# Full attention: SyncE issues the transfers of the maxima's rows, and the maxima are turned three steps before a group's end

## The chip, the cores and the metric

The program runs on one core of a Trainium2 chip. The metric is the device time of one launch, in microseconds (us). Engines: PE is TensorE (PEld its weight loads), DVE is VectorE, ACT is ScalarE, POOL is GpSimd, SP is SyncE, which in this kernel only issues transfers.

## What is computed

Four layers on 4 sequences of 1024 tokens with 128 channels: full attention, an expert feed-forward layer, causal full attention, and a stack of windowed attention and feed-forward layers. The change is inside the two full attentions (the second is causal), which have 16 heads of 8 channels:

```python
scores = jnp.einsum('bhtd,bhsd->bhts', q, k) * scale
attn = jax.nn.softmax(scores.astype(jnp.float32), axis=-1).astype(q.dtype)   # first one
y = jnp.einsum('bhts,bhsd->bhtd', attn, v)
...
scores = jnp.where(causal, scores, -jnp.inf)                                 # second one
attn = jax.nn.softmax(scores / jnp.sqrt(jnp.float32(hd)), axis=-1)
ctx = jnp.einsum('bhqk,bhkd->bhqd', attn, v)
```

## The kernel before

`attention` is called twice, with tags `a1` (not causal) and `a2` (causal). It works on 16 groups (`GROUPS`), each of 4 heads (`GH`) of one sequence. A softmax needs each query's largest score before the exponentials. So every group is gone through twice.

The first pass finds the maxima. For each chunk of 128 queries by up to 512 keys PE multiplies (L456, tile `a_pr`, three PSUM banks used in turn) and DVE takes the largest value per query (L371, into `a_mpart`). There are 64 chunks per group in `a1`, all 512 keys wide, and 48 in `a2`, 128 to 512 wide. Then `finish_maxima` (L376) merges them into the column tile `a_mcol`, PE turns that into rows (`turn_maxima`, L466), and DVE splits the rows into three bf16 parts (L380 to L386, tile `a_mrow`, semaphore `m_split`). Three transfers put them into three spare rows of the group's query tile `a_QS` (`rows_of`, L591, semaphore `m_stored`). With the matching rows of -1 in `a_KS` the second product gives scores minus their maximum.

The second pass makes the output in steps. In `a1` there are 16 steps per group (NS), one for each half of the queries (512) and each block of 128 keys. In `a2` there are 12 steps, with 512, 384, 256 and 128 queries in steps 0 to 3, 512 in steps 4 to 8, and 384, 256 and 128 in steps 9 to 11. A step has scores for two pairs of heads (PE, L474, tile `a_ps`), two exponentials (ACT, L612, tile `a_probs`), and the weighting by the values (PE, L492, tile `a_po`). PE computes the scores of step s+1 inside step s.

The two passes are interleaved by hand: while group g's steps run, the chunks of the group that comes next are spread over them. `turn_steps` gives the order in which steps get chunks: before, the last two steps of the group before (NS-2 and NS-1), then steps 0 to NS-3. The last of that order gets none. After it the maxima are turned. In `a1` the shares are 4 or 5 chunks a step and step 13 has none. In `a2` step 9 has none. Each engine runs its queue in order:

- ACT calls `rows_of` ahead of the exponentials of step NS-2. It waits there for `m_split` and issues the three transfers.
- PE waits for `m_stored` at the start of step NS-1, whose first work is the scores of the next group's step 0.
- SP loads a group's operands (L324 to L326) into one of three buffers once all scores of the group that held the buffer are computed.
- PE's chunk k+3 waits until DVE has read chunk k, for there are three banks. The turned maxima and the turned outputs take a place in the same round of banks.

Of the kernel before, what the change touches and what calls it, by code (L numbers as in the profile page):

```python
# [18 lines left out]
P = 128  # L19
# [221 lines left out]
def attention(nc, A, tag, vals, attn, q_parts, k_parts, ident, causal):  # L241

    PAIRED, BUFS = 2, 3
    with ExitStack() as ctx:
# [32 lines left out]

        turn_steps = [NS - 2, NS - 1, *range(NS - 2)]
        room = [CH - steps[s][2] for s in turn_steps[:NS - 1]]
# [9 lines left out]
        for s in turn_steps:  # L289
            ring += [("chunk", k) for k in share[s]]  # L290
            if s == 1:
                ring.append(("out", 0))
            if s == ends[0] + 1:
                ring.append(("out", 1))
            if s == NS - 3:
                ring.append(("rows", 0))
# [18 lines left out]
        with nc.Block() as block:  # L315
            @block.sync
            def _(sp):
                sp.dma_start(cmask[:, :, :], A["c_causal"]).then_inc(consts, 16)
                sp.wait_ge(zeroed, 4 + FIRST)
                qg = q_parts.rearrange("(g h d) j t -> g (d j) h t", h=GH, d=HD)  # L320
                kg = k_parts.rearrange("(g h d) j t -> g (d j) h t", h=GH, d=HD)

                def load(g, b):
                    sp.dma_start(QS[0:KROWS, b, :, :], qg[g, :, :, :]).then_inc(operands[b], 16)  # L324
                    sp.dma_start(KS[0:KROWS, b, :, :], kg[g, :, :, :]).then_inc(operands[b], 16)
                    sp.dma_start(QS[KROWS:KROWS + 3, b, :, :], norows[:, :, :]).then_inc(operands[b], 16)  # L326

                for g in range(BUFS):
                    load(g, g)
                for g in range(BUFS, GROUPS + 1):  # L330
                    sp.wait_ge(scores, 2 * NS * (g - BUFS + 1) + FIRST)
                    load(g % GROUPS, g % BUFS)

            @block.gpsimd
# [21 lines left out]
            def _(dve):  # L356
# [49 lines left out]
                def step(s, g, v):  # L406
                    if s == 2:
                        normalise(g * 2 - 1, 1, place((g + (GROUPS - 1)) % GROUPS))
                    if s == ends[0] + 2:
                        normalise(g * 2, 0, place(g))  # L410
                    for k in share[s]:
                        half_max(k, v + 1)
                    if s == NS - 3:
                        finish_maxima(v + 1)
# [3 lines left out]
                finish_maxima(0)  # L418
                for s in (NS - 2, NS - 1):
                    for k in share[s]:  # L420
                        half_max(k, 1)
                for s in range(NS - 2):
                    step(s, 0, 0)
                with dve.Fori(0, (GROUPS - 1) // BUFS) as i:
                    for b in range(BUFS):
                        v = i * BUFS + (b + 1)
                        for s in turn_steps:
                            step(s, v - 1 if s >= NS - 2 else v, v)
                normalise(GROUPS * 2 - 1, 1, place(GROUPS - 1))

            @block.tensor
            def _(pe):
# [74 lines left out]
                def step(s, g, b, v, vb, loads):  # L507
                    hq, kt, c0 = steps[s]
                    todo = list(share[s])
                    pe.wait_ge(exped, g * (2 * NS) + (2 * s + 1) + FIRST)  # L510
                    if s == NS - 2:
                        pe.wait_ge(operands[vb], loads * 48)
# [23 lines left out]
                    if s == ends[0] + 1:  # L536
                        turn_out(g * 2, 1, g)
                    if s == NS - 3:
                        turn_maxima(v + 1)
# [8 lines left out]
                pe.wait_ge(operands[1], 48)  # L548
                for s in (NS - 2, NS - 1):
                    for k in share[s]:  # L550
# [3 lines left out]
                for pair in range(PAIRED):  # L554
                    score(0, 0, 0, pair)
                for s in range(NS - 2):
                    step(s, 0, 0, 0, 1, 1)
                with nc.Fori(0, (GROUPS - 1) // BUFS, engines=bass.OrderedEngineSet([pe.engine]),
                             hint_back_edge=True) as i:
                    for b in range(BUFS):  # L560
                        v = i * BUFS + (b + 1)
                        for s in turn_steps:
                            if s >= NS - 2:
                                step(s, v - 1, b, v, (b + 2) % BUFS, i + (1 + (b + 2) // BUFS))
                            else:
                                step(s, v, (b + 1) % BUFS, v, (b + 2) % BUFS, None)
                for s in (NS - 2, NS - 1):
                    kt = steps[s][1]
# [16 lines left out]
            def _(act):  # L585
                def rows_of(par, g):

                    act.wait_ge(m_split, g + 1 + FIRST)
                    for j in range(3):
                        r = KROWS + j  # L590
                        act.dma_start(QS[r:r + 1, par, :, :].rearrange("p h t -> p (h t)")  # L591
                                      .rearrange("p (r c) -> p r c", c=P),
                                      mrow[:, j, :]).then_inc(m_stored, 16)

                def keep_out(u, before):
# [4 lines left out]
                def step(s, g, b):  # L600
                    hq, kt, c0 = steps[s]
                    if s == NS - 2:
                        rows_of((b + 1) % BUFS, g + 1)
                    for pair in range(PAIRED):
# [11 lines left out]
                act.wait_ge(ones_set, 1 + FIRST)  # L616
                rows_of(0, 0)
                for s in range(NS):
# [5 lines left out]
                keep_out(GROUPS * 2 - 1, GROUPS * NS)  # L624
                act.wait_ge(m_stored, (GROUPS + 1) * 48)

# [1424 lines left out]
```

## Time and profile before

| | us |
|---|---|
| Time, median of 3 runs (6683.9 to 6689.47) | 6685.75 |
| The profiled execution's own time | 6694.51 |
| Its span | 6692.6 |
| PE busy in it | 5291.4 (79%) |
| DVE busy | 4489.2 (67%) |
| ACT busy | 3324.6 (50%) |
| Mean granted clock of PE | 0.881 |

The profile is of one execution. Times in it count from the start of its span. The first attention's groups run from about 174 to 1104 us, the second's from about 1402 to 2112 us. A timeline row gives start, length, engine, line, operation, the tile written and the tiles read, and how many are merged in the row. In brackets is how long the engine sat idle before the first of them, and what ended that. "issue" says that the profile shows nothing waited for, which also holds where an engine's queue was at a wait or at issuing a transfer that the row doesn't name. ACTq and SPq are transfers issued by ACT and SP. PEclk is the share of full clock that PE was granted (1.00 is 2.4 GHz, 0.50 is 1.2 GHz).

### The profile page before, as it was taken

Reading aid. Unit: us, or ns where it says so; the run is one execution under the profiler, and the core shown is the slowest. Engines: PE = TensorE matmul, PEld = TensorE weight load, DVE = VectorE, ACT = ScalarE, POOL = GpSimd, SP = SyncE. Lnnn points to the kernel's source line nnn. Section 1 sums busy time; section 2 is a strip of 40 time slices with the busy share of each in tenths; the row PEclk is TensorE's granted clock in tenths of the full one; section 3 lists DMA queues with packets and bytes.
Section 4 is the critical chain, followed back from the end, with each engine's and each line's share of the span. In section 5 each row is a group of like instructions: output and inputs, shape, how many; then the busy total and the mean of one; then the engine's idle time right before and its main releaser. Section 6 shows DMA issues by size and latency. Waiting matters only on the chain. (4 is left out here: it accounts for less than half of the span.)

```text
span 6692.6 us, 227324 instructions
## 1 busy us (share of the span) xinstructions
PE 5291.4 (79%) x94976; PEld 3161.9 (47%) x95234; DVE 4489.2 (67%) x9665; ACT 3324.6 (50%) x6837; POOL 2664.5 (40%) x2369
## 2 busy tenths in 40 slices
PE   5888888667776688888888888887888888888876
PEld 1222222223332455555555565565565565565553
DVE  5777775665665567666667666666666666766764
ACT  1555555324443355555555555555555555555543
POOL 0000000000000556655655655655655655655652
PEclk9999998879998788888888888888888888888886
DMA  3000000211011000010001100110001000110000
GB/s 105 11 15 15 15 15 29 77 27 21 17 21 45 20 25 20 24 41 20 24 25 29 31 25 20 31 35 20 24 25 34 25 25 21 32 32 22 21 26 20
DMA packets 88389, 185.96 MB, mean 28 GB/s; under 512 B 18294, under 2 KB 44854, under 8 KB 87606
## 3 DMA queue, kind: packets, MB, share of 16 engines
q1 hardware_dynamic: 83324, 182.95, 10.4%
q8 instruction: 95, 1.56, 0.1%
q10 hardware_dynamic: 4896, 0.84, 0.1%
q14 instruction: 74, 0.61, 0.0%
HBM read 54.14 MB, written 27.26 MB: 12 GB/s over the span
## 5 line engine op out<-in xcount | busy, mean ns | idle before, releaser
L371 DVE TENSOR_REDUCE a_mpart<-a_pr 128x1 f32<-128x512 f32 (+2 forms) x1904 | 1104.8, 628 | 481.6 <-PE a_pr L456 274.2
L612 ACT ACTIVATE a_probs<-a_ps 128x1024 f32<-128x1024 f32 (+3 forms) x896 | 802.1, 932 | 909.2 <-PE a_ps L474 439.8
L1502 ACT ACTIVATE w_probs<-w_pa,w_nm,w_rqs 128x64 f32<-128x64 f32 x3072 | 968.3, 414 | 125.8 <-DVE w_nm L1650 125.8
L1495 ACT ACTIVATE w_sq<-w_pr 128x512 f32<-128x512 f32 x768 | 466.0, 607 | 901.4 <-DVE w_sinb L1638 901.4
L474 PE MATMUL a_ps<-a_QS,a_KS 128*128 128x512 bf16 (+3 forms) x1719 | 501.0, 374 | 276.6 <-ACT a_probs L612 151.9
L1424 PE MATMUL w_pr<-w_xc,w_w 128*128 128x256 f32 (+1 forms) x1152 | 459.5, 580 | 295.9 <-issue 295.9
L456 PE MATMUL a_pr<-a_KS,a_QS 128*128 128x512 bf16 (+3 forms) x1815 | 609.3, 381 | 91.8 <-DMA a_QS<-a_norows 78.2
L1238 POOL TENSOR_TENSOR w_probs<-w_probs,w_rden 128x512 f32<-128x512 f32 x384 | 393.2, 1045 | 541.1 <-DVE w_rden L1660 541.1
L1212 POOL TENSOR_TENSOR w_sinb<-w_sinb,w_tabk 128x512 f32<-128x512 f32 x384 | 488.2, 1271 | 283.9 <-DVE w_sinb L1638 283.9
L338 POOL COPY a_V<-a_vals 128x288 f32 (+1 forms) x32 | 14.3, 455 | 1436.9 <-PE a_po L492 1436.8
L1638 DVE STREAM_SHUFFLE w_sinb<-w_pr 128x512 f32<-128x512 f32 x768 | 562.4, 732 | 0.0
L1384 PE MATMUL w_pa<-w_probsT,w_V 32*64 32x32 f32 x24576 | 502.9, 228 | 16.4 <-issue 16.4
L1547 ACT COPY w_oT<-w_pa 128x512 f32<-128x512 f32 x384 | 197.1, 600 | 634.3 <-PE w_pa L1384 634.3
L1384 PE MATMUL w_pa<-w_probsT,w_Vp 32*64 32x32 f32 x24576 | 501.3, 228 | 11.7 <-issue 11.7
L1424 PEld LDWEIGHTS w_pr<-w_xc,w_w 128*128 128x128 f32 (+1 forms) x1152 | 311.5, 279 | 418.0 <-issue 374.1
L1384 PEld LDWEIGHTS w_pa<-w_probsT,w_Vp 32*64 32x64 f32 x24576 | 486.5, 132 | 33.5 <-issue 33.5
L1220 POOL TENSOR_TENSOR w_ksum<-w_cosb,w_sinb 128x512 f32<-128x512 f32 x384 | 487.7, 1270 | 36.4
L1220 POOL TENSOR_TENSOR w_qT<-w_cosb,w_sinb 128x512 f32<-128x512 f32 x384 | 487.1, 1269 | 36.4
L1212 POOL TENSOR_TENSOR w_sinb<-w_sinb,w_tabq 128x512 f32<-128x512 f32 x384 | 487.0, 1268 | 9.0 <-DVE w_sinb L1638 9.0
L1384 PEld LDWEIGHTS w_pa<-w_probsT,w_V 32*64 32x64 f32 x24576 | 467.2, 132 | 17.6 <-issue 17.6
L492 PE MATMUL a_po<-a_probs,a_V 128*32 128x512 f32 (+3 forms) x3584 | 456.3, 580 | 3.1 <-issue 0.2
L456 PEld LDWEIGHTS a_pr<-a_KS,a_QS 128*128 128x128 bf16 x1904 | 186.0, 102 | 566.2 <-DVE a_mpart L371 357.0
(225 smaller groups left out, 9928.1 us busy)
## 6 DMA issues: line engine op xcount, KB each, us to landing
w_Vp<-w_V SPq DMA_DIRECT2D x192, 384.0 KB, 3.7
w_Vp<-w_V SPq DMA_DIRECT2D x192, 128.0 KB, 3.4
a_QS<-q_parts SPq DMA_DIRECT2D x34, 384.0 KB
a_KS<-k_parts SPq DMA_DIRECT2D x34, 384.0 KB
q_parts<-a1p_part SPq DMA_DIRECT2D x48, 128.0 KB, 1.8
k_parts<-a1p_part SPq DMA_DIRECT2D x48, 128.0 KB, 1.8
q_parts<-a2p_part SPq DMA_DIRECT2D x48, 128.0 KB, 1.8
k_parts<-a2p_part SPq DMA_DIRECT2D x48, 128.0 KB, 1.8
```

Of the source, the lines that this page charges most:

```text
L371: nc.vector.reduce_max(mpart[:, h, qt, kc:kc + 1], p_r[:, at["chunk", k] % 3, 0:width], AX_X).then_inc(max_read, 1)
L456: mm = nc.tensor.matmul(p_r[:, bank, 0:width], QS[:, b, h, qt * P:(qt + 1) * P], KS[:, b, h, kc * CH:kc * CH + width], start=True, stop=True)
L474: mm = nc.tensor.matmul(p_s[:, pair, e, c0:CH], KS[:, b, h, kt * P:(kt + 1) * P], QS[:, b, h, q0:(hq + 1) * CH], start=True, stop=True)
L492: mm = nc.tensor.matmul(p_o[32 * h:32 * h + 32, c0:CH], V[b][:, kt, h, :], probs[:, s % 2, h, c0:CH], start=kt == 0, stop=s in ends, skip_ ...
L612: nc.scalar.activation(probs[:, s % 2, 2 * pair:2 * pair + 2, c0:CH], p_s[:, pair, :, c0:CH], ACT.Exp, scale=SM_SCALE).then_inc(exped, 1)
L1212: nc.gpsimd.tensor_tensor(sinb[:, u % 4, :, :], sinb[:, u % 4, :, :], tab[:, 1:2, :].broadcast_to([P, 2, PAIR]), ALU.mult).then_inc(S[f"si ...
L1220: nc.gpsimd.tensor_tensor((ksum if u < 4 else qT)[:, b:b + 2, :], cosb[:, u % 4, :, :], sinb[:, u % 4, :, :], ALU.add).then_inc(S[f"add{u} ...
L1384: mm = nc.tensor.matmul(o_of(w)[64 * e:64 * e + 64, b, t, :], (V if blk else Vp)[r, t, f:f + DH], probsT[r, 2 * e + gl, t, c, blk, :], sta ...
L1424: mm = nc.tensor.matmul(F_BANK[bank][0:hi - lo, at, :], w1[:, off + lo:off + hi], xc[:, :], start=True, stop=True)
L1495: nc.scalar.square(sq[:, u, :, :], UNIT_BANK[u][:, :, :]).then_inc(S[f"sq{u}"], 1)
L1502: op = nc.scalar.activation(probs[:, g, t, c, :], s_of(g)[:, t, c, :], ACT.Exp, bias=nm[:, g, t, c:c + 1], scale=scale_of(g)[:, t, c:c + 1])
L1638: nc.vector.stream_shuffle(sinb[:, u % 4, :, :].rearrange("p a f -> p (a f)"), UNIT_BANK[u][:, :, :].rearrange("p a f -> p (a f)"), SWAP). ...
```

## The change

`rows_of` moves from ACT's program to SP's. There it stands ahead of the wait for the scores and the load that follow it. A constant LAG = 3 takes the place of the fixed 2: the turn steps are now the last three of the group before and steps 0 to NS-4, so that the step without chunks, and the turn behind it, come one step earlier (step 12 in `a1`, step 8 in `a2`). The wait for a group's operands moves with them to step NS-3; the wait for `m_stored` stays at step NS-1. The final wait for all rows' transfers moves from ACT to SP.

```diff
-    PAIRED, BUFS = 2, 3
+    PAIRED, BUFS, LAG = 2, 3, 3
...
-        turn_steps = [NS - 2, NS - 1, *range(NS - 2)]
+        turn_steps = [*range(NS - LAG, NS), *range(NS - LAG)]
...
-            if s == NS - 3:
+            if s == NS - LAG - 1:
                 ring.append(("rows", 0))
...
+                def rows_of(g):
+                    sp.wait_ge(m_split, g + 1 + FIRST)
+                    for j in range(3):
+                        r = KROWS + j
+                        sp.dma_start(QS[r:r + 1, g % BUFS, :, :].rearrange("p h t -> p (h t)")
+                                      .rearrange("p (r c) -> p r c", c=P),
+                                      mrow[:, j, :]).then_inc(m_stored, 16)
+
                 for g in range(BUFS):
                     load(g, g)
+                rows_of(0)
                 for g in range(BUFS, GROUPS + 1):
+                    rows_of(g - 2)
                     sp.wait_ge(scores, 2 * NS * (g - BUFS + 1) + FIRST)
                     load(g % GROUPS, g % BUFS)
+                rows_of(GROUPS - 1)
+                rows_of(GROUPS)
+                sp.wait_ge(m_stored, (GROUPS + 1) * 48)
...
-                    if s == NS - 3:
+                    if s == NS - LAG - 1:
                         finish_maxima(v + 1)
...
-                    if s == NS - 2:
+                    if s == NS - LAG:
                         pe.wait_ge(operands[vb], loads * 48)
...
-                    if s == NS - 3:
+                    if s == NS - LAG - 1:
                         turn_maxima(v + 1)
...
-                def rows_of(par, g):
-
-                    act.wait_ge(m_split, g + 1 + FIRST)
-                    for j in range(3):
-                        r = KROWS + j
-                        act.dma_start(QS[r:r + 1, par, :, :].rearrange("p h t -> p (h t)")
-                                      .rearrange("p (r c) -> p r c", c=P),
-                                      mrow[:, j, :]).then_inc(m_stored, 16)
...
-                    if s == NS - 2:
-                        rows_of((b + 1) % BUFS, g + 1)
...
-                rows_of(0, 0)
...
-                act.wait_ge(m_stored, (GROUPS + 1) * 48)
```

ACT's queue in `a1`, from its start through the first group. Before (a_osum is the copy of a half's output, a_probs the exponentials):

```order
L591 DMA a_QS<-a_mrow 1x32x128 x3
L612 ACTIVATE a_probs<-a_ps 128x1024
L598 COPY a_osum<-a_po 128x512
L612 ACTIVATE a_probs<-a_ps 128x1024 x16
L598 COPY a_osum<-a_po 128x512
L612 ACTIVATE a_probs<-a_ps 128x1024 x11
L591 DMA a_QS<-a_mrow 1x32x128 x3
L612 ACTIVATE a_probs<-a_ps 128x1024 x4
```

And now:

```order
L614 ACTIVATE a_probs<-a_ps 128x1024
L602 COPY a_osum<-a_po 128x512
L614 ACTIVATE a_probs<-a_ps 128x1024 x16
L602 COPY a_osum<-a_po 128x512
L614 ACTIVATE a_probs<-a_ps 128x1024 x15
```

The transfers that stood ahead of the last two steps' four exponentials are gone, with the wait in front of them.

SP's queue in `a1` after the first three loads, now (before, the loads alone stood there):

```order
L332 DMA a_QS<-a_mrow 1x32x128 x6
L324 DMA a_QS<-q_parts 48x4x1024
L325 DMA a_KS<-k_parts 48x4x1024
L326 DMA a_QS<-a_norows 3x4096
L332 DMA a_QS<-a_mrow 1x32x128 x3
L324 DMA a_QS<-q_parts 48x4x1024
L325 DMA a_KS<-k_parts 48x4x1024
L326 DMA a_QS<-a_norows 3x4096
```

One set of three rows' transfers now stands ahead of each load.

DVE's queue in `a1` from the end of the first group's maxima to the turn of the second's. Before (L371 are the chunks' reductions, L376 to L386 the turn):

```order
L371 TENSOR_REDUCE a_mpart<-a_pr 128x1 x17
L392 RECIPROCAL a_rsum<-a_pr 128x16
L397 TENSOR_TENSOR a_attn<-a_pr,a_rsum 128x4x32
L371 TENSOR_REDUCE a_mpart<-a_pr 128x1 x30
L392 RECIPROCAL a_rsum<-a_pr 128x16
L397 TENSOR_TENSOR a_attn<-a_pr,a_rsum 128x4x32
L371 TENSOR_REDUCE a_mpart<-a_pr 128x1 x17
L376 TENSOR_REDUCE a_mcol<-a_mpart 128x32
L380 CAST a_mrow<-a_pr 32x128
```

And now:

```order
L384 TENSOR_REDUCE a_mpart<-a_pr 128x1 x21
L405 RECIPROCAL a_rsum<-a_pr 128x16
L410 TENSOR_TENSOR a_attn<-a_pr,a_rsum 128x4x32
L384 TENSOR_REDUCE a_mpart<-a_pr 128x1 x30
L405 RECIPROCAL a_rsum<-a_pr 128x16
L410 TENSOR_TENSOR a_attn<-a_pr,a_rsum 128x4x32
L384 TENSOR_REDUCE a_mpart<-a_pr 128x1 x13
L389 TENSOR_REDUCE a_mcol<-a_mpart 128x32
L393 CAST a_mrow<-a_pr 32x128
```

There are 64 reductions either way. Four of them moved from behind the second output to ahead of the first, so the turn comes a step sooner.

## Rows read from the trace of the kernel before

**Rows 1.** Waits of ACT, first attention: engine, line, what it waited for, us, times, longest.

```profile
ACT a_probs L612 <- issue: 90.1, 16, 5.6
```

**Rows 2.** Waits of ACT, second attention.

```profile
ACT a_probs L612 <- issue: 95.7, 16, 6.3
```

**Rows 3.** Timeline of ACT, rows' transfers: groups 0 and 15 of a1, 0 and 9 of a2.

```profile
222.51 1.82 ACTq L591 DMA_DIRECT2D a_QS<-a_mrow  x3
...
1093.83 1.79 ACTq L591 DMA_DIRECT2D a_QS<-a_mrow  x3
...
1437.31 1.81 ACTq L591 DMA_DIRECT2D a_QS<-a_mrow  x3
...
1836.88 1.79 ACTq L591 DMA_DIRECT2D a_QS<-a_mrow  x3
```

**Rows 4.** Timeline of DVE at the end of a group of a1.

```profile
564.52 1.29 DVE L371 TENSOR_REDUCE a_mpart<-a_pr 128x1 f32<-128x512 f32 x2 [0.39 <-PE a_pr L456]
...
568.31 0.69 DVE L371 TENSOR_REDUCE a_mpart<-a_pr 128x1 f32<-128x512 f32 x1 [0.29 <-PE a_pr L456]
...
571.26 0.28 DVE L386 TENSOR_TENSOR a_mrow<-a_mrest,a_mrow 32x128 bf16<-32x128 f32 x1
576.41 1.29 DVE L371 TENSOR_REDUCE a_mpart<-a_pr 128x1 f32<-128x512 f32 x2 [4.87 <-PE a_pr L456]
578.12 0.69 DVE L371 TENSOR_REDUCE a_mpart<-a_pr 128x1 f32<-128x512 f32 x1 [0.42 <-PE a_pr L456]
580.01 2.54 DVE L371 TENSOR_REDUCE a_mpart<-a_pr 128x1 f32<-128x512 f32 x4 [1.21 <-PE a_pr L456]
```

**Rows 5.** Timeline of ACT, PE and SP in the same stretch.

```profile
568.11 1.03 PE L474 MATMUL a_ps<-a_QS,a_KS 128*128 128x512 bf16 x4
...
570.06 0.29 PE L466 MATMUL a_pr<-ident,a_mcol 128*32 128x128 f32 x1
...
573.55 1.94 ACT L612 ACTIVATE a_probs<-a_ps 128x1024 f32<-128x1024 f32 x2 [5.63 <-issue]
...
574.92 1.03 PE L474 MATMUL a_ps<-a_QS,a_KS 128*128 128x512 bf16 x2 [4.57 <-ACT a_probs L612]
...
577.68 0.31 SPq L324 DMA_DIRECT2D a_QS<-q_parts  x1
```

**Rows 6.** Windows: us, each engine's busy time, PEclk, DMA share, GB/s; first one group.

```profile
515.63:573.55 57.92, 50.02 (x260) 14.15 (x265) 42.91 (x73) 32.37 (x34) 0.45 (x1) 0.94 0.09 15
574.90:577.00 2.10, 2.08 (x5) 0.73 (x6) 0.59 (x1) 1.53 (x2) 0.00 (x0) 0.50 0.02 4
579.70:582.00 2.30, 2.30 (x16) 0.66 (x14) 1.99 (x4) 1.02 (x1) 0.00 (x0) 1.00 1.09 175
585.00:590.00 5.00, 5.00 (x31) 1.47 (x29) 4.31 (x8) 3.21 (x4) 0.00 (x0) 1.00 0.00 0
```

**Rows 7.** The rows' transfers, by their tile: us from issue to landing.

```profile
DMA to landing us min/median/max: 1.8/1.9/3.2
```

**Rows 8.** Timeline of ACT, end of a1: its last group's last steps.

```profile
1095.82 1.94 ACT L612 ACTIVATE a_probs<-a_ps 128x1024 f32<-128x1024 f32 x2 [5.62 <-issue]
1098.96 1.94 ACT L612 ACTIVATE a_probs<-a_ps 128x1024 f32<-128x1024 f32 x2 [1.21 <-PE a_ps L474]
```

**Rows 9.** Timeline of DVE and ACT at the end of a group of a2.

```profile
1659.08 0.28 DVE L386 TENSOR_TENSOR a_mrow<-a_mrest,a_mrow 32x128 bf16<-32x128 f32 x1
1663.05 0.51 DVE L371 TENSOR_REDUCE a_mpart<-a_pr 128x1 f32<-128x128 f32 x2 [3.69 <-PE a_pr L459]
...
1667.42 1.02 ACT L612 ACTIVATE a_probs<-a_ps 128x1024 f32<-128x1024 f32 x1 [3.34 <-PE a_ps L478]
1669.77 1.02 DVE L371 TENSOR_REDUCE a_mpart<-a_pr 128x1 f32<-128x384 f32 x2 [1.36 <-PE a_pr L459]
...
1694.99 1.94 ACT L612 ACTIVATE a_probs<-a_ps 128x1024 f32<-128x1024 f32 x2 [1.83 <-PE a_ps L478]
1698.00 1.69 ACT L612 ACTIVATE a_probs<-a_ps 128x768 f32<-128x768 f32 x2 [1.07 <-PE a_ps L478]
```

More of the change, by code:

```diff
@@ L418, in _ @@
                 finish_maxima(0)
-                for s in (NS - 2, NS - 1):
+                for s in range(NS - LAG, NS):
                     for k in share[s]:
                         half_max(k, 1)
-                for s in range(NS - 2):
+                for s in range(NS - LAG):
                     step(s, 0, 0)
@@ L427, in _ @@
                         for s in turn_steps:
-                            step(s, v - 1 if s >= NS - 2 else v, v)
+                            step(s, v - 1 if s >= NS - LAG else v, v)
                 normalise(GROUPS * 2 - 1, 1, place(GROUPS - 1))
@@ L548, in _ @@
                 pe.wait_ge(operands[1], 48)
-                for s in (NS - 2, NS - 1):
+                for s in range(NS - LAG, NS):
                     for k in share[s]:
@@ L555, in _ @@
                     score(0, 0, 0, pair)
-                for s in range(NS - 2):
+                for s in range(NS - LAG):
                     step(s, 0, 0, 0, 1, 1)
@@ L562, in _ @@
                         for s in turn_steps:
-                            if s >= NS - 2:
+                            if s >= NS - LAG:
                                 step(s, v - 1, b, v, (b + 2) % BUFS, i + (1 + (b + 2) // BUFS))
@@ L566, in _ @@
                                 step(s, v, (b + 1) % BUFS, v, (b + 2) % BUFS, None)
-                for s in (NS - 2, NS - 1):
+                for s in range(NS - LAG, NS):
                     kt = steps[s][1]
```

## The prediction

> **What bounds the kernel now.** Only the two full attentions change, so I read them alone. First the waits of ACT: in the first attention its exponentials stood idle 16 times, 90.1 us in all, on "issue" [rows 1]; in the second 16 times, 95.7 us [rows 2]. Sixteen is the number of groups, and 90.1 / 16 = 5.63 us is what one timeline row shows directly ahead of the exponentials of step 14, from 567.92 to 573.55 [rows 5]. That is a wait of ACT's queue for the split maxima, 3.6 us up to 571.54, followed by 1.79 us of issuing three transfers [rows 3, 4]. Next the distance from one group's transfers to the next: (1093.83 - 222.51) / 15 = 58.09 us in a1 and (1836.88 - 1437.31) / 9 = 44.40 us in a2 [rows 3].
>
> Is ACT's stall on the path? ACT is busy only 32.37 us of a group of 57.92, DVE 42.91, PE 50.02 [rows 6]. Away from the boundary DVE's reductions run with gaps of 0.29 to 0.39 us only, and PE is busy all the time [rows 4, 6], so DVE and PE pace the steps together. At the boundary both stop. DVE ends its last chunk at 568.31 + 0.69 = 569.00 and the split at 571.26 + 0.28 = 571.54, and has its next chunk at 576.41, after 4.87 us of nothing [rows 4]. PE stands 4.57 us until ACT's first exponential, which could have started soon after the scores of 568.11 but starts at 573.55 [rows 5]. So the stall is on everyone's path. It also leaves PE at half clock (0.50, 1.2 GHz), where it had 1.00 again from 579.70 on [rows 6]; in that stretch DVE waits another 0.42 and 1.21 us [rows 4].
>
> **The change, part by part.** I call S the moment at which the maxima are split.
>
> *ACT's wait and issues go.* In a1 the exponentials of the step behind the turn follow their scores, PE goes straight on, and the chunks of that step are in their banks while DVE still splits. From 569.00 to the reduction at 580.01 DVE is idle or in the turn for 7.41 + 0.42 + 1.21 = 9.04 us [rows 4]. The turn itself, 2.54 us (569.00 to 571.54), stays, and so does one ordinary gap of 0.39 us. 9.04 - 2.54 - 0.39 = 6.1 us per group. What is late next is again the reductions, at their ordinary pace. Bounds: 4.6 us if only PE's idle time goes and the clock gives nothing back, 6.6 us if the gaps near the turn close too. I take 6.1, the sum of rows, for it leaves each ordinary gap in.
>
> *The turn one step earlier.* It removes no instruction. It gives the transfers two steps with chunks of cover before PE wants them at step NS-1. Three issues take 1.79 us on ACT [rows 3]; I take the same on SP, since its loads' issue rows are of this kind, and landing takes 1.9 us (1.8 to 3.2) [rows 7]: they are in place at S + 3.7, at worst S + 5.0. In a1 a step of four chunks takes 2.53 + 0.39 = 2.9 us and one of five 3.9; PE enters the first when the turn's product is out (570.35 [rows 5]), 1.2 us before S, so it asks at -1.2 + 2.9 + 3.9 = S + 5.6. It does not wait. In front of the transfers SP has only the load of the group before, issued some 50 us earlier and finished within a few us (DMA share 1.09 at 579.7 to 582, 0.00 from 585 on) [rows 6]. Behind them on SP stands the next load, which had to wait for the last scores anyway; it is needed a whole group later.
>
> *a2, where the last steps are narrow.* Before, from S (1659.36) to the first exponential of step 0 (1667.42) it takes 8.06 us, in which steps 10 and 11 have 8 chunks, with DVE idle 3.69 us at once, and 1.36 us once more ahead of step 0's first chunk [rows 9]. After, steps 9, 10 and 11 come behind the turn with 12 chunks: four of 128, four of 256 and four of 384 keys, at 0.26, 0.38 and 0.51 us [rows 9], 4.6 us of reductions. With some 1.4 us of gaps they end at S + 6.0, and the first exponential of step 0 is at about S + 5.7: 2.4 us gained. The rest of the group took 44.40 - 8.06 = 36.3 us. It has one step less now (1698.00 - 1694.99 = 3.0 us [rows 9]) and 0.5 us less of half clock, but one more chunk to reduce (up to 0.9 us), and a widest step without chunks (step 8 in place of 9), whose wider products and weighting delay the turn by 0.4 us. So 2.4 + 3.0 + 0.5 - 0.9 - 0.4 = 4.6, or 5.5 if the chunk fits into gaps; I take 5.0 us per group. Bounds: 3.7 (the 3.69 us gap alone) and 6.5. PE asks for the rows at S + 5.0 here: covered by 1.3 us at the median landing, not at all at the longest.
>
> *The ends.* The last group has no next one's chunks in its last steps. Its stall goes too (5.62 us idle, of which at least 0.9 is the ordinary wait for scores, so 4.7), and about 1 us of slow clock, but one more step runs bare: 1098.96 - 1095.82 = 3.1 us [rows 8]. That is a gain of 2.6 us. At the start four more chunks are reduced before the first step, and one step less runs in the first group, which cancels. The same for a2. SP's final wait for the transfers is over long before the last output.
>
> *Sum.* a1: 15 x 6.1 + 2.6 = 94. a2: 15 x 5.0 + 2.6 = 78. Together 172 us: 6694.5 - 172 = 6522.5 for a profiled execution. That one ran 8.8 us above the median of the runs shown (6685.75), so I forecast 6514 us. The bounds taken together are 15 x (4.6 + 3.7) + 5 = 130 and 15 x (6.6 + 6.5) + 6 = 203: 6556 and 6483.
>
> **Rivals.**
>
> *The wait for the landed rows takes over.* PE asks at S + 5.6 and S + 5.0. If SP needs longer per issue or rows land later than ACT's did, say at S + 7 in both, PE waits 1.4 and 2.0 us, 32 times: 54 us lost, 6568. For it: the longest landing of 3.2 us [rows 7] would use up a2's cover. Against: the median is 1.9, and the load's data moves later.
>
> *Only the issue time is saved.* If the split and the landing stay ahead of the same work, because they bound the group's end all along, just ACT's 1.79 us of issuing goes, 32 times: 57 us, 6629. Against it: PE waits for ACT's exponential, not for a transfer [rows 5], and the turn is moved too. The Trainium skill's page "DMA: Bandwidth & Descriptors", section "Issuing engines are not separate DMA queues", says that the issuing engine only matters for the sequencer's time to initiate a transfer, which is usually small beside the transfer. By that rule this rival would be the forecast; the trace agrees that the transfer itself gets no faster, but shows a wait of 3.6 us in front of the issues that leaves the exponentials' queue with them.
>
> *The gain is larger.* PE and DVE are both near their pace; if the warm clock also closes gaps later in the group, 7.2 us a group are possible: 30 x 7.2 = 216, 6470. For it: half clock reaches into the next group's first steps [rows 6, 9]. Against: from 579.70 on the clock is 1.00.
>
> *Slower: the rows land with the load.* Rows and operands now share SP's queue. SP issues the load once the last scores are done, some 3.5 us behind S by my estimate (it was 577.68 - 574.92 = 2.8 us into the step behind the stall [rows 5]), and its data keeps the DMA engines busy for about 5 us [rows 6]. If rows were only reported landed when that load is through, at about S + 10.5, PE would wait 4.9 us in a1 and 5.5 in a2, at half clock again behind it (1.6 us), and one wait would be traded for another: 6.5 and 7.1 lost against 6.1 and 5.0 gained, 15 x 2.5 = 37 us slower, 6723. It decides from a landing of about S + 9.3 on. Against: the three transfers of 8 KB are issued ahead of the load and take 1.9 us. The Trainium skill's same page, section "Queues, rings and completion order", says that on each DMA engine descriptors are consumed in ring order. By that the rows go first and this rival falls; no row here has both on one queue.
>
> **How the numbers follow.** Forecast 66%, late landing 14%, issue time only 5%, larger gain 12%, slower 3%. The likeliest gives 6514. The range is 6478 to 6562: the bounds of the sum (6483, 6556), widened a little towards the larger gain and the milder part of the late landing. About 0.2% (13 us) can be told from no change. No case lies within it but a mix near the slower one: faster 96%, same 1%, slower 3%.
>
> **What would show it.** Right: ACT has no idle on issue near a group's end; DVE starts the next chunk within 0.2 us of S; PE's clock stays at 1.00 through a group of a1; the distance between groups' transfers is 52.0 us in a1 and 39.4 in a2; the transfers start at S on SP, about 5 us ahead of PE's need. Wrong: PE's scores released by the rows' transfer (late landing), a clock that still falls at the boundary, or distances above 54 and 41 us.

## The result

| | median, us | runs | lowest to highest |
|---|---|---|---|
| before | 6687.28 | 4 | 6683.90 to 6689.47 |
| after | 6575.98 | 4 | 6569.84 to 6583.24 |

The ratio is 0.9834, with a 95% interval of 0.9817 to 0.9851: the change makes the kernel 111 us faster. The forecast was 6514 us, 172 us faster, with a range that ended at 6562. The sign was right, and ACT's stall went as forecast, but a third of the forecast gain didn't come, and the time fell outside the range.

Between the two profiled executions (6694.51 and 6569.84 us) the gain is 124.7 us. The first attention's stage has 51.1 us of it, the second's 67.1, and 6.4 us lie in the layers around them. Forecast were 94 and 78 for the two. Below, "the period of a group" is the distance from one group's last split instruction on DVE to the next one's, the mean of the 15 regular groups of a traced stage:

| period of a group, us | a1 | a2 |
|---|---|---|
| before | 58.09 | 44.39 |
| forecast | 52.0 | 39.4 |
| after, mean | 54.84 | 40.35 |
| after, groups without the loop's end | 54.40 | 39.63 |
| after, each third group (4 of the 15) | 55.9 to 56.2 | 41.3 to 42.9 |

So a2 was forecast well but for every third group, and a1 misses 2.4 us in every group and 1.6 us more in every third.

### The profile page after: what moved, and what is told of

The parts are those of the page before. It is cut to its first block and busy times, and to the rows that moved or that the text cites. A ratio compares the mean times of both kernels' runs of the same rounds, so it can differ in the third digit from the quotient of the medians.

```text
span 6568.0 us, 227546 instructions
## 1 busy us (share of the span) xinstructions
PE 5262.7 (80%) x95234; PEld 3137.7 (48%) x95234; DVE 4491.0 (68%) x9665; ACT 3325.5 (51%) x6837; POOL 2665.3 (41%) x2369
## 5 line engine op out<-in xcount | busy, mean ns | idle before, releaser
L469 PE MATMUL a_pr<-a_KS,a_QS 128*128 128x512 bf16 (+2 forms) x1904 | 616.0, 371 | 96.6 <-DMA a_QS<-a_norows 77.8
L351 POOL COPY a_V<-a_vals 128x288 f32 (+1 forms) x32 | 14.3, 456 | 1344.9 <-PE a_po L505 1344.8
L1288 PE MATMUL w_pr<-XS,w_wq 128*128 (+1 forms) x1536 | 387.0, 394 | 80.0 <-ACT w_sq L1495 59.3
L505 PE MATMUL a_po<-a_probs,a_V 128*32 128x512 f32 (+3 forms) x3584 | 437.2, 560 | 0.7 <-ACT a_probs L614 0.7
```

The source lines that it names most:

```text
L469: mm = nc.tensor.matmul(p_r[:, bank, 0:width], QS[:, b, h, qt * P:(qt + 1) * P], KS[:, b, h, kc * CH:kc * CH + width], start=True, stop=True)
L505: mm = nc.tensor.matmul(p_o[32 * h:32 * h + 32, c0:CH], V[b][:, kt, h, :], probs[:, s % 2, h, c0:CH], start=kt == 0, stop=s in ends, skip_ ...
```

## The profile after

The page's first part: busy time, share of the span and instructions of each engine; then its row of the only queue for data that is left (ACT's is gone).

```profile
PE 5262.7 (80%) x95234; PEld 3137.7 (48%) x95234; DVE 4491.0 (68%) x9665; ACT 3325.5 (51%) x6837; POOL 2665.3 (41%) x2369
...
q1 hardware_dynamic: 88220, 183.79, 10.6%
```

The waits of ACT in the first attention, where [rows 1] stood. Columns: engine, tile, line, what it waited for, us, times, longest.

```profile
ACT a_probs L614 <- PE a_ps L487: 411.9, 224, 87.9
```

There is no row on issue any more: the 90.1 us of [rows 1] are gone. SP issues the rows' transfers now. Its timeline has these four for a1 and a2, and the view of the tile gives the landing, as in [rows 7].

```profile
442.13 1.79 SPq L332 DMA_DIRECT2D a_QS<-a_mrow  x3
...
496.52 1.79 SPq L332 DMA_DIRECT2D a_QS<-a_mrow  x3
...
1459.31 1.79 SPq L332 DMA_DIRECT2D a_QS<-a_mrow  x3
...
1498.93 1.79 SPq L332 DMA_DIRECT2D a_QS<-a_mrow  x3
...
DMA to landing us min/median/max: 1.8/1.8/2.9
```

Issue and landing are as forecast. The windows show one regular group of a1, and then a longer stretch of a1 and of a2 (columns as in [rows 6]).

```profile
442.13:496.52 54.39, 48.59 (x265) 13.85 (x265) 43.01 (x73) 32.16 (x34) 0.46 (x1) 1.00 0.09 16
450.00:1000.00 550.00, 487.30 (x2658) 139.04 (x2660) 430.74 (x732) 322.40 (x341) 4.11 (x9) 1.00 0.09 16
1450.00:1900.00 450.00, 376.37 (x2935) 160.07 (x2934) 292.74 (x632) 217.82 (x289) 5.03 (x11) 0.99 0.12 21
```

The group of [rows 6] took 57.92 us at a clock of 0.94. The clock is 1.00 now, the higher of the two levels (2.4 GHz), in a1, as forecast. DVE's work in the group is unchanged (43.01 against 42.91 us), so DVE is idle for 11.4 us of a group where the forecast left 9.1. The boundary itself shows a part of it. This is DVE at the end of a regular group of a1, to be read beside [rows 4].

```profile
493.99 0.22 DVE L389 TENSOR_REDUCE a_mcol<-a_mpart 128x32 f32<-128x64 f32 x1
495.34 0.28 DVE L393 CAST a_mrow<-a_pr 32x128 bf16<-32x128 f32 x1 [1.13 <-PE a_pr L479]
...
496.21 0.28 DVE L399 TENSOR_TENSOR a_mrow<-a_mrest,a_mrow 32x128 bf16<-32x128 f32 x1
497.58 1.89 DVE L384 TENSOR_REDUCE a_mpart<-a_pr 128x1 f32<-128x512 f32 x3 [1.09 <-PE a_pr L469]
```

The gap of 4.87 us behind the split has shrunk to 1.09, but it isn't gone: DVE was to go on within 0.2 us. PE's timeline says whom the chunk waited for.

```profile
496.73 0.60 PE L487 MATMUL a_ps<-a_QS,a_KS 128*128 128x512 bf16 x2 [1.43 <-DVE a_mrow L399]
```

PE was held for 1.43 us by the split itself. Its waits over the first attention count 15 of these, and none for the rows' transfer:

```profile
PE a_ps L487 <- DVE a_mrow L399: 21.0, 15, 1.4
```

In every third group the same place looks otherwise. DVE at the end of one of them:

```profile
550.61 0.28 DVE L399 TENSOR_TENSOR a_mrow<-a_mrest,a_mrow 32x128 bf16<-32x128 f32 x1
553.83 2.48 DVE L384 TENSOR_REDUCE a_mpart<-a_pr 128x1 f32<-128x512 f32 x4 [2.94 <-issue]
```

PE's timeline has the three chunks that the banks hold out by 552.72, but DVE starts only at 553.83, 2.94 us behind the split, on "issue". DVE's own `Fori` runs three groups per iteration, and its branch back falls on just these places, four times in each stage (gaps of 2.71 to 3.00 us in a1). And in a2, with the columns as before, the last step of the forecast holds:

```profile
1541.06 0.28 DVE L399 TENSOR_TENSOR a_mrow<-a_mrest,a_mrow 32x128 bf16<-32x128 f32 x1
1541.27 0.47 DVE L384 TENSOR_REDUCE a_mpart<-a_pr 128x1 f32<-128x128 f32 x2
```

DVE goes from the split straight to the next chunks, as was forecast for both. But only two chunks lie ready there. The third one's bank is that of the rows, and PE waits for the split ahead of it. This is PE's wait over a2; no run here takes it away.

```profile
PE a_ps L487 <- DVE a_mrow L399: 9.3, 15, 0.8
```

One more place differs in a1. The planner (the lines of the kernel that fill `share`) put the fifth chunks, for the new order of steps, on steps 14, 2, 6 and 10, where they were on 15, 3, 7 and 11. DVE at steps 0 and 8, behind the copies of the outputs that ACT makes (L602) ahead of its exponentials:

```profile
454.55 0.69 DVE L384 TENSOR_REDUCE a_mpart<-a_pr 128x1 f32<-128x512 f32 x1 [0.53 <-PE a_pr L469]
455.87 2.53 DVE L384 TENSOR_REDUCE a_mpart<-a_pr 128x1 f32<-128x512 f32 x4 [0.63 <-PE a_pr L469]
...
481.40 0.69 DVE L384 TENSOR_REDUCE a_mpart<-a_pr 128x1 f32<-128x512 f32 x1 [0.34 <-PE a_pr L469]
482.71 0.69 DVE L384 TENSOR_REDUCE a_mpart<-a_pr 128x1 f32<-128x512 f32 x1 [0.62 <-PE a_pr L469]
```

This gave three suspects for the missing part. One: the turned maxima sit in the PSUM bank that the next chunk wants. Two: the fetch of DVE's code at its loop's end. Three: where the fifth chunks are. The rival theory was that the rest lies in the transfers or in PE's own pace, so that taking these away gives nothing. The numbers and the edits of the experiments follow; each ratio is to the kernel before, run on the same chip in the same session. Each kernel ran 4 or 5 times, e5_before_hint and e11_before_pad 11 times.

## The experiments

| kernel | what | ratio to before | 95% interval | period a1 / a2, us |
|---|---|---|---|---|
| after | | 0.9834 | 0.9817 to 0.9851 | 54.84 / 40.35 |
| e1_hint | after, DVE's loop end hinted | 0.9803 | 0.9790 to 0.9817 | 54.39 / 39.67 |
| e2_pad | after, rows in another bank | 0.9812 | 0.9799 to 0.9826 | 54.16 / 40.33 |
| e3_share | after, fifth chunks moved | 0.9776 | 0.9763 to 0.9789 | 52.68 / 40.35 |
| e4_lag2 | issued by SP, turn not moved | 0.9826 | 0.9813 to 0.9840 | 53.47 / 41.79 |
| e5_before_hint | before, loop end hinted | 1.0004 | 0.9995 to 1.0013 | 58.10 / 44.37 |
| e6_act_late | turn moved, ACT issues | 0.9839 | 0.9825 to 0.9852 | 54.99 / 40.37 |
| e7_all | after with e1 to e3 | 0.9738 | 0.9725 to 0.9751 | 51.57 / 39.68 |
| e8_wait_kept | e4, ACT's wait kept | 0.9872 | 0.9856 to 0.9887 | 54.62 / 42.25 |
| e9_all_act | e7, issued by ACT | 0.9771 | 0.9758 to 0.9784 | 52.35 / 39.67 |
| e10_all_lag2 | e7, turn not moved | 0.9822 | 0.9808 to 0.9835 | 53.04 / 41.80 |
| e11_before_pad | before, rows in another bank | 1.0000 | 0.9991 to 1.0009 | 58.02 / 44.31 |

### The three suspects, one at a time on the changed kernel

**e1_hint.** The kernel's PE loop has a hint for the branch at its end, DVE's has none.

```diff
-                with dve.Fori(0, (GROUPS - 1) // BUFS) as i:
+                with nc.Fori(0, (GROUPS - 1) // BUFS, engines=bass.OrderedEngineSet([dve.engine]),
+                             hint_back_edge=True) as i:
```

> The changed kernel, with a branch hint for VectorE's loop over groups in both attentions (TensorE's loop has one). Theory A, the loop's back edge: in the changed kernel every third group is longer, 55.97 against 54.40 us in a1 and 42.4 against 39.63 in a2, and there DVE's first chunk behind the turn comes 2.8 to 2.9 us after the split instead of 1.09, since DVE's code at the loop's head is being fetched. With the hint all groups take 54.4 and 39.63 us: 5 x 1.57 + 5 x 2.8 = 22 us less than the changed kernel, about 6554. Theory B, the third groups are longer for something else than DVE's branch (ACT's or SP's queue): no change, 6576.

It measured 0.9803 against after's 0.9834, some 21 us of 6690, though the intervals of the two just touch. The traces decide: a1's long groups are gone (54.3 to 54.4 in all of them), and a2's as well (39.6 to 40.0). Each third group of a1 reads as the others now; this is DVE at such a place.

```profile
385.53 0.28 DVE L399 TENSOR_TENSOR a_mrow<-a_mrest,a_mrow 32x128 bf16<-32x128 f32 x1
386.81 1.89 DVE L384 TENSOR_REDUCE a_mpart<-a_pr 128x1 f32<-128x512 f32 x3 [1.00 <-PE a_pr L470]
```

The gap fell from 2.94 to 1.00 us, and its releaser is a chunk, no longer the issue. Four groups of each stage are at the loop's end, not the five of the expectation: the mean periods fell by 0.45 and 0.68 us, 17 us in 2 x 15 groups. So the cost sits at the branch back at the loop's end. The edit also builds the loop through `nc.Fori`; that call without the hint was not run. The Trainium skill, page "Runtime: NRT & Kernel Launch", section "Instruction fetch mechanics", says that a taken branch to a target that isn't in the buffered pages forces a fetch of the target's page before execution goes on. The trace agrees in kind, with the gap of 2.94 us on issue that the hint takes away. It names only "issue", so that it is the fetch is an inference.

**e2_pad.** The three banks go round over a list of their users. In a1 the list has 64 chunks, two outputs and the rows, 67 entries, and two empty ones at its end make it a multiple of three. The rows' entry is number 66, so bank 0. Behind the two empty entries comes entry 0 of the next round, the first chunk behind the turn: bank 0 again. PE can't start it before DVE has split the rows. The edit puts the empty entries ahead of the rows.

```diff
             if s == NS - LAG - 1:
+                ring += [("none", 0)] * (-(len(ring) + 1) % 3)
                 ring.append(("rows", 0))
```

> The changed kernel, with the two empty places of the round of banks in a1 put ahead of the turned maxima, not behind them, so that the maxima are turned into the bank of the third chunk that follows, not of the first. a2 has no empty places and stays as it is. Theory A: the first chunk's bank is what PE waits 1.43 us for in every group of a1 (waits 21.0 us, 15 times, for a_mrow), ahead of the scores too, and DVE starts 1.09 us after S. Without it DVE starts at S and a group takes 53.3 to 53.6 us instead of 54.4: 12 to 16 us less, 6561 to 6564. Theory B: the steps behind the turn are paced by something else (PE's order), and the gap shows up one burst later: no change, 6576.

The ratio fell by 0.0022 (15 us), within the intervals, so the time alone doesn't show it. The period of a regular a1 group fell from 54.40 to 53.45, and a2's, whose list needs no empty entries, stayed. DVE's timeline behind the split:

```profile
491.83 0.28 DVE L400 TENSOR_TENSOR a_mrow<-a_mrest,a_mrow 32x128 bf16<-32x128 f32 x1
492.04 1.87 DVE L385 TENSOR_REDUCE a_mpart<-a_pr 128x1 f32<-128x512 f32 x3
```

The gap of 1.09 us is gone, and 0.95 of it arrives in the period. But the groups at the loop's end still take 56.0 to 56.3: there DVE's late start hides the bank.

**e3_share.** The fifth chunks go back to steps 15, 3, 7 and 11.

```diff
+        if not causal:
+            k = 0
+            for s in turn_steps:
+                n = 0 if s == NS - LAG - 1 else 5 if s % 4 == 3 else 4
+                share[s] = range(k, k + n)
+                k += n
...
```

> The changed kernel, but in a1 the steps with five chunks are 15, 3, 7 and 11, as before the change, not 14, 2, 6 and 10. Theory A: the two copies of the output (ahead of the second exponentials of steps 0 and 8) keep ACT's exponential back, and a fifth chunk in the step in front of them keeps DVE busy meanwhile; after the change it is one step too early, and DVE's gaps there are 0.53 + 0.63 and 0.34 + 0.62 us in place of 0.39 and 0.30. A group takes 53.1 us instead of 54.4: 20 us less, 6556. Theory B: the place of the fifth chunk doesn't matter, since each costs the same 0.97 us anywhere: 6576.

This is the largest of the three: 0.9776 against 0.9834, 39 us, with intervals that don't meet. The period of a1 fell by 2.16 us, more than the 1.3 us that I had added up from the gaps at steps 0 and 8. DVE at step 0, at step 8, and at the end of the group:

```profile
442.58 1.89 DVE L391 TENSOR_REDUCE a_mpart<-a_pr 128x1 f32<-128x512 f32 x3 [0.32 <-PE a_pr L476]
444.76 2.53 DVE L391 TENSOR_REDUCE a_mpart<-a_pr 128x1 f32<-128x512 f32 x4 [0.29 <-PE a_pr L476]
...
468.76 1.89 DVE L391 TENSOR_REDUCE a_mpart<-a_pr 128x1 f32<-128x512 f32 x3 [0.32 <-PE a_pr L476]
470.94 0.69 DVE L391 TENSOR_REDUCE a_mpart<-a_pr 128x1 f32<-128x512 f32 x1 [0.29 <-PE a_pr L476]
...
482.92 0.28 DVE L400 CAST a_mrow<-a_pr 32x128 bf16<-32x128 f32 x1 [0.74 <-PE a_pr L486]
...
485.17 1.89 DVE L391 TENSOR_REDUCE a_mpart<-a_pr 128x1 f32<-128x512 f32 x3 [1.09 <-PE a_pr L476]
```

The gaps at both steps are 0.29 and 0.32 again. The wait for the turned maxima is 0.74 us where it was 1.13: a second source, which I had left out. This second part is no cost of the change, for the kernel before waited as long:

```profile
570.38 0.28 DVE L380 CAST a_mrow<-a_pr 32x128 bf16<-32x128 f32 x1 [1.13 <-PE a_pr L466]
```

The edit puts a fifth chunk into step 11, right ahead of the turn, where neither kernel has one. The bank's 1.09 us stays, as it should.

### Were these costs there before?

**e5_before_hint** and **e11_before_pad** put the edits of e1 and e2 into the kernel before, each with 11 runs.

> The kernel before the change, with the branch hint for VectorE's loop. Theory A, the change uncovered the back edge: before it, DVE stood idle 4.87 us behind the turn anyway, so that fetching the loop's head (about 2.9 us) was hidden; the hint changes nothing in a1 (58.09 us a group), at most 0.3 us a group in a2 where third groups are 44.9 against 44.1: within 5 us of the kernel before. Theory B, the back edge always cost what it costs after the change: 22 us faster than before.

> The kernel before the change with the empty places of a1's banks ahead of the turned maxima. Theory A: ACT's stall covers this cost, since the first chunk behind the turn came 4.87 us after S anyway; no change, ratio 0.999 to 1.001, a1 58.1 us a group. Theory B, the cost was paid before too: 14 us faster, 0.998.

Neither does anything: 1.0004 (0.9995 to 1.0013) and 1.0000 (0.9991 to 1.0009). DVE in e11_before_pad shows why.

```profile
569.78 0.28 DVE L387 TENSOR_TENSOR a_mrow<-a_mrest,a_mrow 32x128 bf16<-32x128 f32 x1
575.00 1.29 DVE L372 TENSOR_REDUCE a_mpart<-a_pr 128x1 f32<-128x512 f32 x2 [4.94 <-PE a_pr L457]
```

With another bank for the rows, DVE still stands for 4.94 us (4.87 in [rows 4]), since PE waits for ACT. Both costs lay under ACT's stall, and the change brought them up. The placing of the fifth chunks is another matter: the change itself made it.

### Which half of the change does it?

**e4_lag2** leaves the turn where it was and only lets SP issue (`LAG = 2`). **e6_act_late** moves the turn, and ACT issues the transfers at their old place, ahead of the exponentials of step NS-2. The first's edit:

```diff
-    PAIRED, BUFS, LAG = 2, 3, 3
+    PAIRED, BUFS, LAG = 2, 3, 2
```

The second's, in ACT's step (SP's calls of `rows_of` are taken out, and the function stands in ACT's block as before):

```diff
                 def step(s, g, b):
                     hq, kt, c0 = steps[s]
+                    if s == NS - 2:
+                        rows_of((b + 1) % BUFS, g + 1)
```

> The changed kernel with LAG = 2: SP issues the rows' transfers, but the maxima are turned where they were before. Theory A, ACT's stall was nearly all of it: PE now asks for the rows at about S + 2.8 and has them at S + 3.7, a wait of about 1 us a group, partly paid by a1's fifth chunks, which are in the right steps again: a1 about 54.0 us a group, a2 about 40, in all 6565 to 6585. Theory B, the earlier turn carries a good part of the gain, since without it the landing takes the place of ACT's wait (and the clock falls again): a1 above 56, a2 above 42, 6630 or more.

> The changed kernel's earlier turn (LAG = 3), but the transfers issued by ScalarE at step NS-2 as before: it finds the maxima split long since, so it doesn't wait, and only the three issues (1.79 us) stand in front of the exponentials. Theory A, the wait was the cost and the issue a small part: ACT has about 0.9 us of slack a step, so a1 loses 0.5 to 1 us a group against the changed kernel (about 55.5), a2 1 to 2 us, since the rows land about 2.8 us later than from SP; 6600 to 6625. Theory B, the issuing engine's time is most of it: 57 us are lost against the changed kernel or more, 6635 and up.

Either half gives nearly all: 0.9826 and 0.9839, with 0.9834 for both together. e6_act_late (6590.58 us) came out below the expected 6600 to 6625, although ACT does wait, which wasn't expected. The wait is short, 0.8 us, since the split now ends soon after ACT has come to its place. ACT's issues and next exponentials, then DVE at the same place:

```profile
494.67 1.94 ACT L612 ACTIVATE a_probs<-a_ps 128x1024 f32<-128x1024 f32 x2 [0.89 <-PE a_ps L474]
497.42 1.79 ACTq L591 DMA_DIRECT2D a_QS<-a_mrow  x3
499.40 3.90 ACT L612 ACTIVATE a_probs<-a_ps 128x1024 f32<-128x1024 f32 x4 [2.80 <-PE a_ps L474]
...
498.48 1.89 DVE L371 TENSOR_REDUCE a_mpart<-a_pr 128x1 f32<-128x512 f32 x3 [1.09 <-PE a_pr L456]
500.66 2.73 DVE L371 TENSOR_REDUCE a_mpart<-a_pr 128x1 f32<-128x512 f32 x4 [0.30 <-PE a_pr L456]
```

ACT's 5.63 us without work [rows 5] have become 0.8 of waiting (from 494.67 + 1.94 = 496.61 to 497.42) and 1.8 of issuing, and DVE's gaps are those of after: ACT's queue has room for it while PE stands at the rows' bank. In e4_lag2 a1 is even faster (53.47), with its shares those of before, as in e3_share; a2 is slower (41.79), and there PE waits for the rows. This is e4_lag2's wait of PE over a2:

```profile
PE a_ps L487 <- DMA a_QS<-a_mrow: 20.5, 12, 2.3
```

**e8_wait_kept** asks what the 1.79 us of issues alone are worth: e4_lag2 plus ACT's old wait, without its issues.

```diff
+                    if s == NS - 2:
+                        act.wait_ge(m_split, g + 2 + FIRST)
```

> LAG = 2 and the transfers issued by SyncE, but ScalarE still waits for the split maxima ahead of step NS-2's exponentials: of the stall of 5.63 us only the 1.79 us of issuing go. Beside the run with LAG = 2 without that wait (a1 53.5, a2 41.8 us a group) it parts the stall. Theory A, the wait is the larger part: a1 about 56 and a2 about 43 us a group, the clock falls less or not at all, 6620 to 6640. Theory B, the issue is the larger part, as where issuing from one engine or another is what counts: within 10 us of the run without the wait, 6585.

It measured 6612.26 us, 0.9872, below the expected band of 6620 to 6640: the issues alone are worth 86 us of 6698, or 2.7 us in each of 32 groups on the mean (3.5 in a1 and 2.1 in a2 by the periods), not 1.8. That leaves 31 us of e4_lag2's gain to the wait. ACT, PE and DVE at a group's end of a1, and two stretches of its windows, the first right behind PE's gap:

```profile
496.41 3.81 ACT L616 ACTIVATE a_probs<-a_ps 128x1024 f32<-128x1024 f32 x4 [3.80 <-DVE a_mrow L399]
...
497.56 0.60 PE L487 MATMUL a_ps<-a_QS,a_KS 128*128 128x512 bf16 x2 [2.53 <-ACT a_probs L616]
...
498.42 1.89 DVE L384 TENSOR_REDUCE a_mpart<-a_pr 128x1 f32<-128x512 f32 x3 [2.19 <-PE a_pr L469]
```

```profile
497.56:499.00 1.44, 1.44 (x7) 0.52 (x7) 0.58 (x1) 1.44 (x2) 0.00 (x0) 1.00 0.06 12
450.00:1000.00 550.00, 493.08 (x2672) 140.29 (x2673) 432.51 (x737) 326.23 (x344) 3.71 (x9) 0.99 0.09 14
```

PE idles for 2.53 us where it was 4.57 [rows 5], and its clock is 1.00 right behind the gap, where it was 0.50 behind the longer one [rows 6]; over the stretch it is 0.99, where the same stretch of before had 0.94. So in a1 the shorter gap also saves the stretch at half clock behind it. In a2 (1450 to 1900 us) it saves little of it: 0.94 against 0.92. The wait for the split that stays costs little on top of e4_lag2 (1.1 us in a1, 0.5 in a2), for PE had to wait for the split itself there, by the rows' bank (15 times in a1, 21.1 us; 11 times in a2, 5.8 us).

### All three edits, and the halves again

**e7_all** is after with e1, e2 and e3 together.

> The changed kernel with the three single edits together: the hint for VectorE's loop, the empty places of the banks ahead of the turned maxima, the fifth chunks of a1 in steps 15, 3, 7 and 11. Theory A, the three costs add up: a1 51.3 us a group (54.84 less 0.45, 0.95 and 2.16), a2 39.67 (less 0.68), so 15 x 3.55 + 15 x 0.68 = 63 us less than the changed kernel, about 6515. Theory B, they share a cover (the gap behind the turn hides one of them): 52 us or more in a1, 6530.

0.9738 (0.9725 to 0.9751), the fastest kernel here, 64 us below after by the ratios. The periods are 51.57 and 39.68 us, where 52.0 and 39.4 were forecast. DVE behind a split in a1:

```profile
425.18 0.28 DVE L401 CAST a_mrow<-a_pr 32x128 bf16<-32x128 f32 x1 [0.74 <-PE a_pr L488]
...
426.05 0.28 DVE L407 TENSOR_TENSOR a_mrow<-a_mrest,a_mrow 32x128 bf16<-32x128 f32 x1
426.26 1.87 DVE L392 TENSOR_REDUCE a_mpart<-a_pr 128x1 f32<-128x512 f32 x3
```

The single gains in a1's mean period add up to 0.45 + 0.68 + 2.16 = 3.29, and together they give 3.27. By the ratios they add up to 74 us and give 64, within their intervals. What remains open is why each third group of a1 still takes 52.2 to 52.7 us beside 51.27. In these groups it is PE that is late: its next scores start 0.85 us behind the turn's product (372.68 to 373.53), where 0.12 is usual (424.86 to 424.98). PE's own loop, which has the hint, also ends there, but e9_all_act has no such groups.

**e9_all_act** and **e10_all_lag2** take one half of the change out of e7_all: the first issues from ACT by the edit of e6_act_late, the second has `LAG = 2` as e4_lag2.

> The three edits together (hint, empty places, fifth chunks) on the earlier turn, but with the rows' transfers issued by ScalarE at step NS-2. Theory A, with the earlier turn it does not matter who issues: ACT finds the maxima split and has slack for 1.79 us; the same as with SyncE within 0.2%, ratio to the kernel before 0.974 to 0.976. Theory B, on the tighter pace ACT's 1.79 us show: 1 us a group or more in a1, ratio 0.977 or above.

> The three edits together and SyncE as issuer, but the maxima turned in the old place (LAG = 2). Theory A, with the gap behind the turn gone PE reaches the wait for the landed rows earlier: it asks at about S + 2 and they are in place at S + 3.6, so a1 takes about 52.8 us a group instead of 51.6 and a2 about 40.8 instead of 39.7: 30 to 40 us slower than the three edits with LAG = 3, ratio 0.979 to 0.980. Theory B, the earlier turn is worth nothing here either, as for the changed kernel without the edits: 0.974.

Now both halves count: 0.9771 and 0.9822 against 0.9738, with intervals that don't meet. e9_all_act's ratio is the one that its second theory gave. Its groups are 0.8 us longer in a1 and no longer in a2, which is 12 of the 22 us between the ratios; the other 10 aren't explained. With the bank free there is nothing left in a1 for ACT's issues to hide beside. e10_all_lag2 is 56 us behind e7_all where 30 to 40 were expected, for a2 took 41.8 us and not 40.8. ACT, then PE, then DVE of e9_all_act at a group's end:

```profile
480.22 1.94 ACT L621 ACTIVATE a_probs<-a_ps 128x1024 f32<-128x1024 f32 x2 [1.20 <-PE a_ps L483]
482.97 1.80 ACTq L600 DMA_DIRECT2D a_QS<-a_mrow  x3
484.95 3.90 ACT L621 ACTIVATE a_probs<-a_ps 128x1024 f32<-128x1024 f32 x4 [2.80 <-PE a_po L501]
...
486.20 0.60 PE L483 MATMUL a_ps<-a_QS,a_KS 128*128 128x512 bf16 x2 [0.99 <-ACT a_probs L621]
...
487.05 1.89 DVE L379 TENSOR_REDUCE a_mpart<-a_pr 128x1 f32<-128x512 f32 x3 [1.11 <-PE a_pr L465]
```

ACT waits 0.8 us for the split (480.22 + 1.94 = 482.16 to 482.97) and issues for 1.8, its exponentials come late by both, PE waits 0.99 us for them, and DVE 1.11 for PE. In e10_all_lag2 it is the landing. PE's waits over a1:

```profile
PE a_ps L496 <- DMA a_QS<-a_mrow: 16.1, 15, 1.5
```

Fifteen groups, 1.07 us each, and in a2 12 waits of 1.8: the rival of the late landing, true where the turn is two steps from the end and not where it is three.

## Why the prediction was wrong

Point by point, by its own steps:

- *ACT's wait and issues go.* Right. No idle time on issue is left, PE's clock is 1.00 in a1 where 0.94 was, and e8_wait_kept shows that the issues alone carried 86 us, with the clock. The wait carried 31, though it was 3.6 us of the stall of 5.63 and the issues 1.79: with ACT's wait gone, PE waits for the split at the rows' bank.
- *PE goes straight on, and the chunks of that step are in their banks while DVE still splits.* This step failed in a1. PE was held 1.43 us by the rows' bank and DVE idled 1.09 us. The rule that "PE's chunk k+3 waits until DVE has read chunk k" and that the rows take a place in that round stood ahead of the prediction; which bank that is was not worked out. e2_pad gives 0.95 us back, and e11_before_pad shows that it cost nothing before. In a2 the step held for DVE, while PE was held by the third chunk's bank, 9.3 us in 15 waits.
- *What is late next is the reductions, at their ordinary pace.* This failed too, and cost most. The ordinary pace of before belonged to its shares. The turn's earlier step made the planner shift the fifth chunks by one step, away from the steps just ahead of ACT's copies of the outputs. e3_share gives 2.16 us a group back. Not all of that was missing: 54.40 - 0.95 - 2.16 = 51.29 is 0.7 below the forecast 52.0, and 0.39 of it is the turn's wait, which before had too. So of the 2.4 us missing in every group of a1 the bank has 0.95 and the shares about 1.45. I had counted the moved chunks for a2, and in a1 only their number.
- *A cost that no term held:* DVE's loop end, 1.7 us on the mean in every third group of a1 and 2.7 in a2. e1_hint gives 17 us back by the periods and 21 by the ratio. e5_before_hint shows that before it was free. The question "what is late next" was answered with the reductions, and not with DVE's own supply of instructions.
- *The landing is covered.* Right at three steps in both stages (PE waits for it in no regular group of a1 and once in a2, 0.6 us), and e10_all_lag2 shows why the third step is needed. The prediction says that the trace of before agrees that the transfer gets no faster. No row of that trace could show it; the median of 1.8 us from SP, beside 1.9 from ACT, does.
- *a2.* 5.0 us were forecast, 44.39 - 39.63 = 4.76 came in groups without the loop's end, 4.04 on the mean.
- *The ends and the rest.* 94 and 78 us took in 2.6 us for each stage's ends; they gave 51.1 - 15 x 3.25 = 2.3 and 67.1 - 15 x 4.04 = 6.5. The 6.4 us around the attentions (2.4 between them, 4.0 behind) weren't forecast and aren't explained.

In all, 15 x (54.84 - 52.0) = 42.6 us were missing in a1 and 15 x (40.35 - 39.4) = 14.3 in a2, and the ends and the rest gave some 10 back: 47 of the 47 us between 172 and 124.7. The 13 us from there to the measured 111 are the profiled executions, of which before's lay 7.2 us above its median and after's 6.1 below.

The prediction's own sign of being wrong, a distance above 54 us in a1, was met with 54.84. Of the rivals, "only the issue time is saved" (6629) and "slower" (6723) fell, as did "the gain is larger": rows issued by SP ahead of the load landed in 2.9 us at most. "The wait for the landed rows takes over" had a time near the measured one (6568) and the wrong cause. The range was too narrow because all its bounds came from gaps that the trace of before showed; none allowed for a wait that the removed stall was covering.

## What to carry to other kernels

When a stall is removed, list everything that happens beside it, not only the work that waits for its end: which buffer the next work needs, where that engine's loop branches, and which operations stand around it on each queue. The rows' bank and the loop's end were free under a gap of 4.87 us, and the placing of the fifth chunks came with the change. Together the three took back 64 of the 175 us that e7_all gains. When a change moves a step through a planner, compare what the planner gives to every step, and not only around the moved one. A test of one half of a change tells little while another wait covers the difference: e6_act_late and e9_all_act hand the issues back to ACT alike, worth nothing beyond the intervals in the one and 0.0033 of the time in the other.

## What the runs showed of the hardware

At the branch back at the end of its loop DVE stood idle for 2.94 us on issue between a split and chunks that lay ready by then, and with the hint the gap was 1.00 us, all of it a wait for a chunk. Three transfers of rows took ACT's or SP's queue 1.8 us, in either case, and landed a median of 1.8 to 1.9 us after their issue. A gap of 2.53 us in each group of a1 left PE's mean clock at 0.99, with 1.00 right behind the gap; one of 4.57 us left it at 0.94, with 0.50 behind it.
